# A graph attention layer with a routed feed-forward on one core: masks, residual and normalisation move to GpSimd, transposed copies change sides

## What is computed

```python
q = (x @ Wq).reshape(N, HEADS, DH)
k = (x @ Wk).reshape(N, HEADS, DH)
v = (x @ Wv).reshape(N, HEADS, DV)
scores = jnp.einsum('nhd,mhd->hnm', q * SCALE, k)
scores = jnp.where(adj[None, :, :] > 0, scores, NEG_INF)
attn = jax.nn.softmax(scores, axis=-1)
sat = jnp.einsum('hnm,mhd->nhd', attn, v).reshape(N, V_DIM)
out = jnp.concatenate([sat[:SIZE_U] @ weightr, sat[SIZE_U:] @ weightd], axis=0)
out = out + bias
return jax.nn.leaky_relu(out, negative_slope=0.01)
...
gate_scores = x @ Wg + bg
_, idx = jax.lax.top_k(gate_scores, K)
mask = jax.nn.one_hot(idx, E, dtype=x.dtype).sum(axis=-2)
...
h = jax.nn.gelu(jnp.einsum('td,edh->teh', xf, W1) + b1[None], approximate=False)
y = jnp.einsum('teh,ehd->ted', h, W2) + b2[None]
out = jnp.einsum('ted,te->td', y, mf)
```

## Time and profile before

| | us |
|---|---|
| median of 3 runs | 852.59 |
| the runs | 851.79 to 852.61 |
| the profiled execution | 851.31 |
| its span, first to last instruction | 849.5 |
| busy in the span: PE / DVE / ACT / POOL | 811.7 / 639.2 / 679.0 / 195.5 |
| preparation and first score tile | 0 to about 53 |
| attention steps with all parts | about 53 to 633 |
| attention step without new scores | about 633 to 657 |
| feed-forward | about 657 to 849 |

### The profile page before, as it was taken

How to read it: one execution, slowest core, us unless ns; L and a number is a source line. 1 busy time by engine, 2 the same in 40 slices (tenths; PEclk the granted TensorE clock), 3 DMA queues, 4 the chain that set the end, 5 groups by cost and what they waited for, 6 DMA issues and landing times.

```text
span 849.5 us, 31821 instructions
## 1 busy us (share of the span) xinstructions
PE 811.7 (96%) x12080; PEld 597.7 (70%) x12080; DVE 639.2 (75%) x1530; ACT 679.0 (80%) x1099; POOL 195.5 (23%) x209
## 2 busy tenths in 40 slices
PE   4969999999999999999999999999997889999997
PEld 2537777777777777777777777777776567777775
DVE  6597888888888888888888888887883465555555
ACT  4838887878788888878888888788885789999996
POOL 4180000100100010000001000000000566766774
PEclk9979999999999999999999999999999999999999
DMA  8515433443343334434333443443100000000000
GB/s 220 110 25 91 81 58 58 66 74 58 56 77 59 56 61 72 65 56 69 67 56 58 68 71 56 63 72 56 31 0 2 1 14 14 14 14 12 12 12 12
DMA packets 40900, 44.96 MB, mean 53 GB/s; under 512 B 22168, under 2 KB 32160, under 8 KB 40864
## 3 DMA queue, kind: packets, MB, share of 16 engines
q0 software_dynamic: 9216, 33.56, 24.6%
q1 hardware_dynamic: 31216, 10.71, 5.4%
q10 hardware_dynamic: 432, 0.20, 0.1%
HBM read 71.72 MB, written 2.10 MB: 87 GB/s over the span
## 4 chain that ended last, share of the span: by engine, by line
PE 73%; POOL 14%; issue 8%; DVE 3%; DMA 1%; ACT 0%; POOLq 0%; DVEq 0%
PE ps L912 28%; PE ps L881 19%; PE ps L896 19%; POOL prob L349 14%; PE ps L923 2%; PE ps L837 1%; PE ps L842 1%; PE ps L850 1%; DVE prob L589 1%; PE ps L931 1%; PE ps L828 1%; DMA x_sb<-in_x 1%; DVE stats L513 0%; POOLq L348 0%; ACT prob L418 0%
## 5 line engine op out<-in xcount | busy, mean ns | idle before, releaser
L589 DVE CUSTOM_DVE_ANT_0 prob<-ps,mask 128x1024 f32<-128x1024 f32 x256 | 311.8, 1219 | 90.1 <-PE ps L881 84.4
L418 ACT ACTIVATE prob<-prob,nmax 128x1024 f32<-128x1024 f32 x256 | 292.8, 1144 | 9.9 <-DVE nmax L597 9.9
L912 PE MATMUL ps<-pt,v_sb 128*64 128x128 f32 x4096 | 253.2, 277 | 0.0
L912 PEld LDWEIGHTS ps<-pt,v_sb 128*64 128x64 f32 x4096 | 222.4, 137 | 13.4 <-issue 7.5
L433 ACT ACTIVATE pt<-ps 128x1024 f32<-128x1024 f32 x128 | 131.1, 1024 | 113.0 <-PE ps L896 113.0
L896 PEld LDWEIGHTS ps<-ident,prob 64*128 64x128 f32 x4096 | 152.6, 139 | 78.5 <-issue 78.4
L881 PE MATMUL ps<-k_half,q_row 64*128 64x512 f16 x1536 | 189.7, 380 | 5.0 <-DVE low L589 5.0
L896 PE MATMUL ps<-ident,prob 64*128 64x64 f32 x4096 | 183.7, 229 | 9.4 <-issue 4.7
L349 POOL TENSOR_TENSOR prob<-prob 128x512 f16<-128x512 f32 x104 | 122.6, 1183 | 57.1 <-ACT prob L483 54.4
L294 POOL DMA_DIRECT2D mask<-in_adj x64 | 35.4, 553 | 429.2 <-DVE low L589 429.2
L791 DVE SCALAR_TENSOR_TENSOR x_sb<-ps,k_half,x_sb 128x128 f32 (+1 forms) x256 | 72.5, 344 | 78.1 <-PE ps L1029 76.8
(11 more groups left out here) (97 smaller groups left out, 670.8 us busy)
## 6 DMA issues: line engine op xcount, KB each, us to landing
mask<-in_adj POOLq DMA_DIRECT2D x64, 512.0 KB, 5.5
q_row<-q_nat SPq DMA_DIRECT2D x128, 32.0 KB, 4.7
x_sb<-in_x SPq DMA_DIRECT2D x4, 512.0 KB, 7.0
out<-x_sb SPq DMA_DIRECT2D x8, 256.0 KB, 2.3
pt<-in_L_ffn_W SPq DMA_DIRECT2D x1, 1024.0 KB, 6.5
wq_sb<-in_L_gnn_Wq ACTq DMA_DIRECT2D x1, 64.0 KB, 2.9
wk_sb<-in_L_gnn_Wk ACTq DMA_DIRECT2D x1, 64.0 KB, 4.5
wv_sb<-in_L_gnn_Wv ACTq DMA_DIRECT2D x1, 64.0 KB, 5.7
```

The lines of the kernel that those rows point to most:

```text
L418: act.activation(prob[:, h, cols], prob[:, h, cols], ACT.Exp, bias=nmax[:, h:h + 1], scale=-1.0, accum_out=sums[:, j, h, p:p + 1]).then_in ...
L589: dve.tensor_tensor_reduce(out=prob[:, h, col_of(p)], in0=ps[:, 2 * (u % 2):2 * (u % 2) + 2, :].rearrange("p b c -> p (b c)"), in1=mask[:, ...
L912: ins = pe.matmul(ps[dims, AV, 0:P], v_sb[:, tile, dims], pt[:, UNITS.index((h, p)), t, :], start=(tile == 0), stop=(tile == NT - 1))
```

## The change

- **Masks.** `make_mask` goes from DVE to GpSimd: the mask tile is read as int16, and max(value, 0) + (-0x2080) turns the bit patterns of 0.0 and 1.0 into those of -2^64 and 2^-65.
- **Copies.** The halves are swapped: DVE and ACT share the even units, ACT alone copies the odd ones. `mask_scores` of an odd unit waits for T(u) of the tile before, since `prob` is overwritten.
- **Small work on DVE.** `finish_tile` stands ahead of unit 2; the rest stands behind the even maskings (u = 0, 4, 6), `keep_logits` a step later. `divide` writes back to PSUM, and `leaky` becomes two instructions that read PSUM.
- **GpSimd** also takes `residual`, the epsilon, and `normalise` in two instructions, for all pairs but the last.
- **Weights.** The raw feed-forward weights lie in `x2t_hi` and `x2t_lo`; GpSimd splits them in 16 parts of 128 columns, one an even step (one part ahead of step 1), by tensor_tensor with a broadcast factor. ACT's `x2t_high` waits for the part it overwrites.
- **V.** `xn_t` lies in `pt` with all eight chunks; V is projected in steps 0 (five chunks) and 1 (three), through one PSUM bank.
- **PE.** attend stands ahead of `x2_transpose` and `logits`. The gate ranking of the first 28 tiles moves from ahead of the last step into it, behind unit 2.

The diff, cut:

```diff
+            def make_mask(i, par, c):
+
+                pool.wait_ge(adj_in[par][c], 8 * i - 8 * par + 16)
+                pool.nop(nofuse=True)
+                part = mask[:, par, c * HALF:(c + 1) * HALF].bitcast(I16)
+                pool.tensor_scalar(part, part, 0, MASKED, ALU.max, ALU.add).then_inc(mask_ready, 1)
...
+            def split_weights(done, raw, pair):
+
+                rows, cols = raw.shape
+                pool.tensor_tensor(raw, raw, factor[0:rows, 0:1].to_broadcast([rows, cols]), ALU.mult).then_inc(w_split_chain, 1)
+                pool.wait_ge(w_split_chain, done + 1)
+                pool.tensor_tensor(pair[:, 0, :], raw, factor[0:rows, 1:2].to_broadcast([rows, cols]),
+                                   ALU.mult).then_inc(w_split_chain, 1)
+                pool.wait_ge(w_split_chain, done + 2)
                 pool.tensor_tensor(pair[:, 1, :], raw, pair[:, 0, :], ALU.subtract).then_inc(w_split_chain, 1)
...
+            def split_ffn_part(t0):
+
+                part = bass.ds(t0 * W_PART // PAIR, W_PART)
+                split_weights(3 * t0 + W_SPLITS - 6 if not isinstance(t0, int) or t0 > 0 else 0,
+                              w1_raw[:, part], w1_pair[:, :, part])
+                split_weights(3 * t0 + W_SPLITS - 3 if not isinstance(t0, int) or t0 > 0 else 3,
...
+            def residual(t0):
+
+                pool.wait_ge(post_chain, POST_STEPS // PAIR * t0 + POST_STEPS)
+                rows = bass.ds(t0, PAIR)
+                pool.tensor_tensor(x_sb[:, rows, :], x_sb[:, rows, :], o_act[:, :, :], ALU.add).then_inc(x1_ready, PAIR)
+
+            def inverse_std(t0):
+
+                pool.wait_ge(stats_chain, 2 * X_PARTS + t0 + PAIR)
+                pool.nop(nofuse=True)
+                pool.tensor_scalar(ve2[:, :], mv2[:, :, 1], EPS, 0.0, ALU.add, ALU.add).then_inc(ve2_ready, PAIR)
+                pool.wait_ge(ve2_ready, t0 + PAIR)
+                pool.tensor_tensor(rstd2[:, :], ve2[:, :], expo[:, 0:PAIR], ALU.pow).then_inc(rstd2_ready, PAIR)
+
+            def normalise(t0):
+
+                mean = mv2[:, :, 0:1].to_broadcast([P, PAIR, D])
+                pool.tensor_tensor(x_mid[:, :, :], x_sb[:, bass.ds(t0, PAIR), :], mean, ALU.subtract).then_inc(x_mid_ready, PAIR)
+                pool.wait_ge(rstd2_ready, t0 + PAIR)
+                pool.wait_ge(x_mid_ready, t0 + PAIR)
+                pool.tensor_tensor(x2[:, :, :], x_mid[:, :, :], rstd2[:, :].unsqueeze(2).to_broadcast([P, PAIR, D]),
+                                   ALU.mult).then_inc(x2_ready, PAIR)
+
+            def step(i, par, post=True, ahead=True, load=True, split=True):
+
+                if ahead:
+                    make_mask(i + 1, 1 - par, 0)
+                if post and par == 0:
+                    inverse_std(i - 4)
+                    normalise(i - 4)
+                if load:
+                    load_adj(i + 2, par, 0)
+                if split and par == 0:
+                    split_ffn_part(i)
+                if ahead:
+                    make_mask(i + 1, 1 - par, 1)
+                if post and par == 1:
+                    residual(i - 3)
+                if load:
+                    load_adj(i + 2, par, 1)
+
...
                 act.wait_ge(transposed, NU * j + u + 1)
                 if not early:
                     act.wait_ge(av_done, NP * j + p - 3)
-                elif u == 4:
-                    act.wait_ge(w_split_chain, 6)
-                if u % 2:
+                if u % 2 == 0:
...
-            def mask_scores(i, par, u):
+            def mask_scores(i, par, u, prior):
 
                 h, p = UNITS[u]
+                if u % 2 and prior:
+                    dve.wait_ge(transposed, NU * i - NU + u + 1)
                 if u in (0, 4):
                     dve.wait_ge(mask_ready, 2 * i + u // 4 + 1)
...
                     second = t * HEADS * D + D
-                    ins = dve.scalar_tensor_tensor(o_pre[:, t, :], ps[:, bank, second:second + D], rinv[:, t, 1:2],
+                    ins = dve.scalar_tensor_tensor(ps[:, bank, second - D:second], ps[:, bank, second:second + D], rinv[:, t, 1:2],
                                                    o_half[:, t, :], ALU.mult, ALU.add)
                 link(ins)
...
+            def leaky(t0, bank=POST):
+
+                pre = ps[:, bank, :].rearrange("p (t c) -> p t c", t=PAIR)[:, :, 0:D]
+                link = linker(post_chain, POST_STEPS // PAIR * t0 + 4)
+                link(dve.tensor_scalar(o_neg[:, :, :], pre, 0.0, SLOPE, ALU.min, ALU.mult))
+                dve.scalar_tensor_tensor(o_act[:, :, :], pre, 0.0, o_neg[:, :, :], ALU.max, ALU.add).then_inc(post_chain, 1)
...
-            def step(i, par, prior=True, now=True, finish=True, post=True, ahead=True, early=False):
+            def step(i, par, prior=True, now=True, finish=True, post=True, ready=True, early=False, last=False):
 
                 for u in range(NU):
-                    if prior and u % 2:
+                    if finish and u == 2:
+                        finish_tile(i - 2, par)
+                    if prior and u % 2 == 0:
                         copy_pt(i - 1, u, early)
                     if now:
-                        mask_scores(i, par, u)
+                        mask_scores(i, par, u, prior)
                         if u in (5, 7):
                             row_max(i, u // 7, u)
-                    if u == 1 and finish:
-                        finish_tile(i - 2, par)
-                    if ahead and u in (3, 7):
-                        make_mask(i + 1, 1 - par, u // 4)
                     if post and par == 1:
-                        if u == 1:
+                        if u == 0 and ready:
+                            keep_logits(i - 5)
+                        if u == 0:
                             invert_sums(i - 3)
-                        if u == 3:
+                        if u == 4:
                             divide(i - 3)
-                        if u == 5:
+                        if u == 6:
                             leaky(i - 3)
-                        if u == 7:
-                            residual(i - 3)
                     if post and par == 0:
-                        if u == 1:
+                        if u == 0:
                             statistics(i - 4)
-                        if u == 3:
-                            normalise(i - 4)
-                        if u == 5:
+                        if u == 6:
...
                     if now:
                         scores(i, par, 2 * k)
                         scores(i, par, 2 * k + 1)
+                    if not prior:
+                        project_v(k)
+                    if not prior and k == 3:
+                        project_v(k + 1)
                     if prior:
                         transposes(i - 1, 2 * k + 1, early)
+                    if early and k < NC - V_FIRST:
+                        project_v(V_FIRST + k)
                     if post and par == 1 and k == 1:
                         out_project(i - 3)
+                    if k >= AV_BLOCK and prior:
+                        attend(i - 1, k - AV_BLOCK, early)
+                    elif k < AV_BLOCK and drain:
+                        attend(i - 2, k + NP - AV_BLOCK)
                     if post and par == 0 and k == 2:
                         x2_transpose(i - 4)
                     if post and par == 0 and k == 3:
                         logits(i - 4)
-                    if k >= AV_BLOCK and prior:
```

More of the change, by code:

```diff
@@ L343, in ffn @@
+            step(NT - 1, 1, load=False, ahead=False)
+            step(NT, 0, load=False, ahead=False, split=False)
+            inverse_std(NT - PAIR)
             def ffn(j, par):
@@ L410, in _ @@
                     normalise_x(2 * p + 5)
+            for j in range(V_FIRST):
+                copy_v(j)
             def exp_unit(j, u):
```

155 lines of the change are left out of this document (71 added, 84 removed).

## The result

The changed kernel takes **856.16 us** (median of 6 runs, 855.21 to 858.14); the kernel before, run beside it, 852.19 (6 runs, 851.21 to 852.8). The ratio is 1.0049, with a 95% interval of 1.0035 to 1.0063: slower by half a per cent, where 842.0 was predicted, in a range of 834 to 850. Both the direction and the range were wrong.

The account below looks back on a forecast made before the run. PE was taken as the bound, losing 0.56 us a pair to waits for ACT's full copy. Gains of 8.0 + 1.5 + 1.2 = 10.7 us take the profiled 851.3 to 840.6, median 841.9 (say 842), range 834 to 850.

Parts of the forecast that it names:

- Masks on GpSimd: Attention loop: each GpSimd mask instruction takes 1.9 us, bound 1.9 to 4.7; GpSimd sums to 15.3 us a pair, all hidden.
- Rival A: Attention loop: GpSimd becomes the bound, kernel slower; at 8 us a mask, 885 us in all; chance 0.11.
- The decision point of rival A: Attention loop: GpSimd's fixed work is 7.7 us a pair, so above 7.3 us a mask instruction it sets the pair.
- the sign for A: Loop pair at 39 us or more, GpSimd's mask over 7 us, DVE idle before maskings by mask_ready.
- The rule on the shared port: Changed loop: DVE instructions with two SBUF inputs or 2-port mode wait for GpSimd's; none seen there, so no term.
- Copies swapped: Attention loop: odd units' transposes no longer wait for ACT's full copy; 8.0 us gained, bounds 0 to 9.7.
- DVE's small work in its new places: Attention loop: between maskings it delays the next copy some 0.1 us once a pair, hidden; upper bound 4 us lost.
- Start: Preparation and first tiles: V projections moved later, first scores at 38.5 for 41.22; 1.5 us gained, between -1 and 5.
- Last attention step and tail: Kernel's end: 1.3 and 0.7 us gained in the step, 0.8 lost in the tail; 1.2 net, between -1 and 4.
- The sum: Whole kernel: 8.0 + 1.5 + 1.2 = 10.7 us gained, giving a median of 841.9 us.

## Why the prediction was wrong, step by step

- *Masks on GpSimd*: **the step that failed.** "I take 1.9, since it is one input and the same length; 1.9 to 4.7 stays as bound." The row for 1.9 was a mult and add, the bound 4.7 a two-input subtraction; the new instruction is a max and an add, and took 7.09, or 3.46 ns an element, outside both. Rival A named the mechanism ("GpSimd's cost hangs on the operation") and the point from which it decides (7.3 us), and I gave it 0.11 since "every add, multiply or subtract lies at 2.3 ns or less". Of those rows only one was a tensor_scalar, a mult and add, which happens to be a cheap pair; the others have two inputs and say nothing of this one. The figure of the Trainium skill, page "GPSIMD Engine Reference", section "Performance versus the Vector engine", that I cited, 1.8 us by an estimate, holds for mult and add (1.91) and not for max and add; the measurement decides.
- *The decision point of rival A*: mis-sized too. GpSimd's other work, said as 7.7 us a pair, is 37.32 - 4 x 7.09 = 8.96 with the gaps between its instructions. So it becomes the bound at (36.7 - 8.96)/4 = 6.9 us, not at 7.3, and 7.09 lay above it. Nor did it show by mask_ready, as the sign for A said: no masking waited for a mask in the loop, the delay came by residual and statistics. A pair then costs 37.32 for 36.7: the loop kept 4.1 us of what the short masks give in the same stretch, 10.3.
- *The rule on the shared port*: I asked it of the changed loop alone, and found no victim. For the loop that was right: beside the masks of 7.09 us every masking stayed at 1.21 to 1.23 us and every half copy at 0.68 to 0.69. But the same masks run beside the preparation, where DVE's normalise_x is a tensor_scalar with SBUF in and out. The row for it, with 341 ns each, stood beside the ones that I read. This cost 10.9 us, more than the whole loss. With masks of 1.9 us it cost almost nothing, so its size follows from the first step; but that took the gap told above, and the place could have been named.
- *Copies swapped*: right. With the short masks T(odd) starts 1.29 to 1.30 us behind S(even) in 95 of 124 places (all was said; the others are mostly at 1.33 to 1.55), the slots without other work are 4.33 us (4.36 said), the pair 36.70 for 36.8. From the first scores of tile 1 to the last ones of tile 31 that kernel gained 575.58 - 565.24 = 10.3 us for 8.0; of it the 14 pairs from tile 4 on have 9.7 for 7.8.
- *DVE's small work in its new places*: right that it is hidden, and more important than said: with neither it nor the masks off DVE the swap gains 0.12 us a pair.
- *Start*: 1.5 was said. With the short masks it is 0.2 (54.02 for 54.24), with the first masks on DVE 0.0. "exp at 51.3 for 51.87" was 51.77, and there the gain ended, though the scores came 2.6 us sooner. The five copies ahead of it, which I had seen, were worth 3.0 to 4.4 us.
- *Last attention step and tail*: 2.0 and -0.8 were said, 3.0 and -0.7 measured.
- *The sum*, with the price put right, comes near: the profiled execution of the kernel with short masks ends on PE 12.7 us sooner, for 10.7 said, and its median is 839.8 for 841.9. Part of that is luck: the start gave 1.3 us less than said, the loop 2.3 and the last step 1.0 more.

## What to carry to other kernels

Before work goes to GpSimd, look for a row with the same pair of operations, not the same type or length; where there is none, the bound above is open, and the point at which the engine becomes the bound deserves the larger chance. A long GpSimd instruction must be held against every stretch that it can run in, the preparation too, for DVE instructions with SBUF in and out beside it. And before an engine's queue is given up on, try the cheap form of the same arithmetic: here x * 2^64 - 2^64 in place of max and add was worth 16 us with one line.

## What the hardware showed that was not expected

- GpSimd's tensor_scalar over 128x2048: 1.9 us for mult-add, mult-mult and add-mult, 5.4 for one operation alone, 7.1 for every other pair tried, for int16, bf16 and float32 alike where more than one was tried.
- A DVE tensor_scalar of 0.34 us became one of 6.50 (7.09 in the changed kernel) beside an instruction of 7.1. A two-input one from SBUF became 4.49, beside one of 7.08 us and beside one of 4.50 alike; shift, with 8 elements, became 2.90 for 0.16. These two were released 2.0 and 2.6 us before GpSimd's instruction of 7.1 had ended.
- In the kernel with the early exp and the masks on DVE the granted clock (the number behind POOL's) fell to 0.90 and 0.75 where PE, busy 2.76 of 5 us, waits for the gate ranking on DVE; from 634 to 636 it is 0.51, the lower level (1.2 GHz). Its last step took 1.2 us longer than that of the kernel without the early exp. The kernel with the first masks on DVE and that with half the masks on each show the same (0.50 from 642 to 644 and from 636 to 638, the step 1.4 and 1.6 us longer). The changed kernel, that with all masks on DVE and the three with its new order and short masks have the same wait in their profiled executions, and stay at 1.00. What decides is open, so 1 to 2 us of the differences between these kernels may be the clock's.

```profile
630.00:635.00 5.00, 2.76 (x50) 2.58 (x48) 2.05 (x8) 3.43 (x5) 0.00 (x0) 0.90 0.00 0
635.00:640.00 5.00, 4.01 (x58) 3.17 (x56) 1.92 (x5) 2.69 (x6) 0.00 (x0) 0.75 0.01 3
```
